# Seven pairs of x sums moved from the windows of a GRU-and-FFN kernel into its setup

## The reference

```python
for t in range(64):                       # B = 64, D = 512
    gi = x[:, t] @ W_ih + b_ih            # 512 x 1536
    gh = h @ W_hh + b_hh
    r = sigmoid(gi_r + gh_r); z = sigmoid(gi_z + gh_z)
    n = tanh(gi_n + r * gh_n)
    h = (1 - z) * n + z * h
    states[:, t] = h
out = x + ffn(states)                     # fp8-rounded operands, gate/up 1408 wide, silu, down
```

## Time and profile before

| | us |
|---|---|
| median of 3 runs | 2847.83 |
| lowest, highest | 2846.3, 2849.53 |
| the profiled execution | 2844.01 |
| its span | 2842.2 |

### The profile page before, as it was taken

One profiled execution on the slowest core, in us unless ns is written; L12 is line 12 of the kernel. 1 busy time (PEld: TensorE's weight loads), 2 busy tenths in 40 slices (PEclk: granted clock), 3 DMA queues, 4 the chain that ended last, 5 costly groups with the idle time before them and its releaser, 6 DMA issues. The chain is left out here.

```text
span 2842.2 us, 154419 instructions
## 1 busy us (share of the span) xinstructions
PE 2554.6 (90%) x67605; PEld 1655.8 (58%) x67605; DVE 1686.3 (59%) x3398; ACT 1139.7 (40%) x2317; POOL 1252.9 (44%) x598
## 2 busy tenths in 40 slices
PE   2088999999989999999999999999896999999996
PEld 1066777777767778777665664755642444444442
DVE  8852222224822222225737879867492888888887
ACT  1312222225722222225602333323233777777774
POOL 0256666663146666665161450713601233333334
PEclk8599999999999999999999999999998999999998
DMA  6833222224622222225664353443432223232322
GB/s 196 241 82 82 71 72 74 71 71 107 146 69 71 72 74 71 71 75 138 191 143 122 109 144 113 125 153 97 146 121 95 71 86 95 79 96 84 95 64 54
DMA packets 234857, 293.97 MB, mean 103 GB/s; under 512 B 69581, under 2 KB 194023, under 8 KB 233895
## 3 DMA queue, kind: packets, MB, share of 16 engines
q1 hardware_dynamic: 212743, 240.84, 31.3%
q10 hardware_dynamic: 18304, 36.19, 3.7%
q0 software_dynamic: 3680, 15.21, 1.9%
HBM read 231.61 MB, written 60.45 MB: 103 GB/s over the span
## 5 line engine op out<-in xcount | busy, mean ns | idle before, releaser
L1161 PE MATMUL psum<-second_shared 64*32 64x384 f16 x32768 | 1029.5, 325 | 48.1 <-issue 28.3
L1169 PE MATMUL psum<-low_w,low_hot 64*32 64x384 f16 x16384 | 819.1, 325 | 5.6 <-issue 5.6
L1407 DVE TENSOR_SCALAR second_shared<-psum 32x384 f16<-32x384 f32 x496 | 272.4, 549 | 754.1 <-PE psum L1161 746.8
L1161 PEld LDWEIGHTS psum<-second_shared 64*32 64x32 f16 x32768 | 594.5, 93 | 209.6 <-issue 78.8
L971 POOL TENSOR_TENSOR low_hot<-first_shared,sum_mask 128x1024 f16<-128x1024 f16 x256 | 504.5, 1971 | 425.0 <-DVE first_shared L1394 165.4
L965 POOL TENSOR_TENSOR second_shared<-first_shared,whole_mask 128x2048 f16<-128x2048 f16 x128 | 462.3, 3612 | 447.3 <-PE psum L1161 352.3
L1061 ACT ACTIVATE second_shared<-psum 32x384 f16<-32x384 f32 x496 | 239.4, 483 | 807.5 <-PE psum L1161 801.5
L1249 PE MATMUL psum<-low_w,low_hot 64*64 64x384 f16 x12288 | 513.9, 325 | 12.6 <-issue 6.5
L1249 PEld LDWEIGHTS psum<-low_w,low_hot 64*64 64x64 f16 x12288 | 373.9, 108 | 146.2 <-issue 10.0
L1169 PEld LDWEIGHTS psum<-low_w,low_hot 64*32 64x32 f16 x16384 | 315.7, 93 | 66.3 <-issue 7.1
L2037 PE MATMUL psum<-first_shared,hT 128*64 128x256 f32 (+1 forms) x1856 | 314.6, 492 | 0.0
(11 more groups left out here) (286 smaller groups left out, 2667.5 us busy)
## 6 DMA issues: line engine op xcount, KB each, us to landing
low_w<-w_rows SPq DMA_DIRECT2D x384, 144.0 KB
low_w<-w_rows SPq DMA_DIRECT2D x256, 120.0 KB
second_shared<-w_rows SPq DMA_DIRECT2D x1024, 24.0 KB, 1.8
x_gates<-x_out ACTq DMA_DIRECT2D x58, 384.0 KB, 2.4
xg<-x_gates SPq DMA_DIRECT2D x58, 384.0 KB, 3.2
low_w<-w_rows SPq DMA_DIRECT2D x256, 72.0 KB
low_w<-w_rows SPq DMA_DIRECT2D x384, 48.0 KB
w_rows<-quantised SPq DMA_DIRECT2D x24, 384.0 KB, 4.9
```

Of the source, the lines that this page charges most:

```text
L1161: last = nc.tensor.matmul(run[m][u][j * Q:(j + 1) * Q, :], whole_hot[rows[u], m, sign, kk, j % 2 * Q:(j % 2 + 1) * Q], whole_w[rows[u], m, ...
L1169: nc.tensor.matmul(run[m][u][j * Q:(j + 1) * Q, :], low_hot[rows[u], m, kk, j % 2 * Q:(j % 2 + 1) * Q], low_w[rows[u], m, at:at + UC], sta ...
L1407: last = nc.vector.tensor_scalar(whole_w[u * B:u * B + Q, m, 0, bq, :], run[m][u][bq * Q:(bq + 1) * Q, :], 1.0 / HIGH_ONE, None, ALU.mult)
```

## The change

Seven of the 29 pairs are made in the setup, with the first four chunks of `raw` as weights and with PSUM banks 1, 3, 4, 5 and 0, after the two plain sums have been taken out of PSUM. The windows keep 5, 6, 5 and 6 pairs. To make room on ScalarE, the 48 loads of operand rows go to SyncE, behind the writes of chunks 2 to 5, and eight activations that fill `whole_a` go from the end of the setup to its start. The first four loads of x rows, which ScalarE issued at the start of the second block, are issued at the start of the kernel. VectorE adds the bias to both plain sums in chunk 0.

```diff
+            X_SETUP = 7
+            SETUP_BANKS = x_banks(1, (3, 4), (5, 0))
# SyncE, setup, in the loop over the chunks n, behind the writes W0, W1, W2
+                            if n == 2:
+                                sp.wait_ge(pieces_out, PIECES_OUT)
+                                load_low(sp, 0, LOW_ROWS, ROWS_X0)
+                            elif n == 3:
+                                load_whole(sp, 0, 0, ROWS_X0)
+                            elif n == 4:
+                                sp.wait_ge(pieces_out, 2 * PIECES_OUT)
+                                load_low(sp, H0, LOW_ROWS, ROWS_H)
+                            elif n == 5:
+                                load_whole(sp, H0, 1, ROWS_H)
# ScalarE, setup
+                        def take_pair(j):
+                            for step in (2 * j, 2 * j + 1):
+                                take_out(a, step, SETUP_BANKS)
+                                if step + 2 < 2 * X_SETUP:
+                                    place_bias(step + 2, SETUP_BANKS)
+                                if step % 2 == 0 and j + 1 < X_SETUP:
+                                    copy_rows(a, j + 1, SETUP_BANKS)
+
+                        for j in range(2):
+                            load_rows(a, j)
+                        a.wait_ge(id_ok, 1)
+                        for m in range(2):
+                            for part in range(2):
+                                own = slice(part * B, part * B + Q)
+                                for bq in range(2):
+                                    nc.scalar.activation(whole_a[own, m, :, bq * Q:(bq + 1) * Q], ident[own, own].unsqueeze(1).to_broadcast([Q, NBK, Q]),
+                                                         ACT.Copy, scale=HIGH_ONE)
...
                             a.wait_ge(w3_ok, n + 1)
                             if n + 2 < CHUNKS:
                                 scale_rows(n + 2)
-                            if n == 2:
-                                a.wait_ge(pieces_out, PIECES_OUT)
-                                load_low(a, 0, LOW_ROWS, ROWS_X0)
-                            elif n == 3:
-                                load_whole(a, 0, 0, ROWS_X0)
...
-                            elif n >= CHUNKS - 2:
...
+                            if n == 0:
+                                copy_rows(a, 0, SETUP_BANKS)
+                                a.wait_ge(x_cleared, 1)
+                                a.wait_ge(bias_ok, 1)
+                                for step in range(2):
+                                    place_bias(step, SETUP_BANKS)
+                            elif n <= X_SETUP:
+                                take_pair(n - 1)
# VectorE, setup, in chunk 0: both plain sums
-                            if c < PLAIN:
-                                v.wait_ge(plain_sum, c + 1)
+                                for n_plain in range(PLAIN):
+                                    v.wait_ge(plain_sum, n_plain + 1)
# TensorE, end of the setup
+                        pe.wait_ge(plain_ok, 2 * PLAIN)
+                        x_pairs(pe, range(X_SETUP), raw[:, 0:KD, :], SETUP_BANKS)
# the windows
-                    return range(X_PAIRS * w // WINDOWS, X_PAIRS * (w + 1) // WINDOWS)
+                    rest = X_PAIRS - X_SETUP
+                    return range(X_SETUP + rest * w // WINDOWS, X_SETUP + rest * (w + 1) // WINDOWS)
# ScalarE, second block
-                        for j in range(2):
-                            load_rows(a, j)
-                            a.wait_ge(x_cleared, t - FINE + 1)
+                            a.wait_ge(x_cleared, t - FINE + 2)
```

More of the change, by code:

```diff
@@ L390, in build @@
                 bias_in = ssem("bias_in")
+                bias_ok = ssem("bias_ok")
                 plain_turned = ssem("plain_turned")
@@ L605, in _ @@
                                 v.wait_ge(bias_in, 64)
-                                nc.vector.tensor_tensor(bias_sum[:], bias[:, 0, 0:2 * HALF], bias[:, 1, 0:2 * HALF], ALU.add)
-                            if c < PLAIN:
-                                v.wait_ge(plain_sum, c + 1)
-                                for at, (tile, part) in enumerate(zip(ps_plain[c % 2], (slice(0, 2 * HALF), slice(2 * HALF, 3 * HALF)))):
-                                    nc.vector.tensor_tensor(gates_plain[:, c, part], tile, bias[:, 0, part], ALU.add).then_inc(plain_ok, 1)
+                                nc.vector.tensor_tensor(bias_sum[:], bias[:, 0, 0:2 * HALF], bias[:, 1, 0:2 * HALF], ALU.add).then_inc(bias_ok, 1)
+                                for n_plain in range(PLAIN):
+                                    v.wait_ge(plain_sum, n_plain + 1)
+                                    for tile, part in zip(ps_plain[n_plain % 2], (slice(0, 2 * HALF), slice(2 * HALF, 3 * HALF))):
+                                        nc.vector.tensor_tensor(gates_plain[:, n_plain, part], tile, bias[:, 0, part], ALU.add).then_inc(plain_ok, 1)
                     @block.tensor
```

## The result

| | before | after |
|---|---|---|
| median of 6 runs, us | 2846.46 | 2861.23 |
| lowest, highest | 2840.84, 2849.53 | 2854.44, 2862.02 |
| the profiled execution | 2844.01 | 2860.68 |
| its span | 2842.2 | 2858.9 |

The changed kernel is 14.8 us slower: the ratio is 1.0054, with an interval of 1.0038 to 1.007. Forecast were 2844.3 and a range up to 2854. It is the second rival's side, and 5 us beyond the rival's own 2856.3.

What follows compares the result with a forecast made beforehand. VectorE's chain was taken to bound the setup and three of four windows, TensorE only the last. +6.0 (setup) - 0.7 (start) + 7.2 (returns) - 16.0 (last window) = -3.5 us, so 2844.3 by median, range 2837 to 2854.

Steps and rivals of the forecast that it cites:

- the second rival: Setup, chunks 4 to 7: full DMA engines make writes land late and VectorE stop; 12 to 20 us, 2856.3; chance 0.18.
- The setup's transfers: Setup: moved x rows and sums add 0.25 to a DMA share of 0.90, so transfers land later; 1.8 us added.
- The whole term of the setup: Setup's end: first x rows, TensorE's new tail and later transfers delay the second block by 6 us, between 4 and 12.
- my three signs of being wrong: Half pair behind the turn at 2.4 GHz, VectorE waiting for writes in the setup, or a pair there over 11.1 us.
- The first x rows: Kernel's start: four loads of 128 KB delay the last weights by up to 1.6 us; 1.3 taken.
- TensorE's tail: Setup: TensorE's seven pairs end at 139.3, so the second block starts at 141.3, 4.2 us later than before.
- The second block's start: TensorE's first product there waits less for its load without the x rows' loads; gain 0 to 2 us, 0.7 taken.
- The three returns of the clock: Steps 2 to 4: after waiting for the state TensorE resumes at 1.2 GHz; 2.4 us each, 7.2 in all.
- The last window: Eight pairs become six, so the block ends with VectorE's state instead of TensorE's sums; gain 15.7 to 16.8 us, 16 taken.
- windows 2 to 4: Windows of steps 2, 3 and 4: VectorE's state ends them, so fewer pairs gain nothing.

Runs made afterwards that it cites:

- small x stores: The changed kernel with the 14 setup stores of x sums cut to 16 of 128 partitions; median 2840.48 us, 0.9982 of the kernel before.
- Full windows: The changed kernel with windows of 7, 7, 7 and 1 pairs instead of 5, 6, 5 and 6; median 2847.7 us, 1.0006 of the kernel before.
- the row loads on SyncE alone: The kernel before with only the 48 row loads moved to SyncE, no x sums in the setup; median 2851.46 us, 1.002 of the kernel before.

## Why the prediction was wrong

**The setup's transfers** are the step that failed: I added 1.8 us for later landings, and took SyncE's late writes "as hidden". The whole term of the setup was +6, and it measured +27.4. The second rival had the mechanism (VectorE stops for `moved`, in chunks 5 to 7, with 20.2 us against its 12 to 20) and its point of decision, a start of 152.3; the start was 164.54. I gave it 0.18. Three readings misled me. I added a share of 0.25 to one of 0.90 and spoke of landings that slip, when the sum says that the bytes don't fit: they take longer, and the writes that VectorE needs stand in the same engines. By my own numbers a share of 1.0 left 8.5 us of the engines' time free in 85, for a need of 20.9: 12.4 us too much, and not the 9 (3 beyond my 6) that I wrote. I gave the landing a spare of 5 to 8 us and took late writes as hidden by it, where chunk 5's writes took 11.6 us from the issue of the last. And I priced SyncE's 16 issues at 0.7 us each, by what they took on ScalarE in a setup without x sums. They took 1.1 us each, so the five spare microseconds were gone before the first write was late. The runs show which is cause and which is effect: the order alone costs nothing (no waits), the order under traffic costs about 6 us, and the stores' traffic taken away leaves 1.4 of 19.7 us. Of my three signs of being wrong, VectorE's waits for writes came, and a pair of more than 11.1 us once (12.1, from 117.01 to 129.13, where TensorE waited for ScalarE); the half pair at 2.4 GHz did not.

The Trainium skill ("DMA: Bandwidth & Descriptors", section "Issuing engines are not separate DMA queues") holds that all issuing engines feed the same 16 DMA engines. The runs agree: moving 48 loads from one queue to another left the start at 137.64. The sentence with it in the prediction put the setup 3 us beyond my 6 if the share could not pass 1.0; from 70 to 130 the largest share of all twelve profiles was 0.94, and a window of 10 us in after reached 0.99.

**The first x rows** were 1.3 us in the sum, by their bytes; they took about 4. Why more than their bytes is not shown.

**TensorE's tail** was right in kind and didn't decide. A pair takes 11.06 us there too (but for the one of 12.1), and the first products are slow (8.35 us for a half pair). The last sums ended at 145.4 instead of 139.3, of which 3.3 are the first x rows' share. The block waited for VectorE. In small x stores, without the waits, the tail does decide, and the setup is then 8.2 us longer than before, against the +6 of the sum.

**The second block's start** was forecast at -0.7. TensorE's wait for the first load went from 8.88 to 7.21 us, 1.7 less. Its first instruction is 27.42 us later than before and the first gates, some 540 us on, are 26.56 us later, so -0.9 is left there.

**The three returns of the clock** were 7.2 us in the sum and took 7.5: the steps from one state to the next grew by 2.1, 3.1 and 2.3. The turns waited 22.36, 11.50 and 22.32, as forecast. Windows of one microsecond behind the turn of step 2 in after (the columns as above):

```profile
1609.00:1610.00 1.00, 0.99 (x4) 0.58 (x6) 0.27 (x1) 0.00 (x0) 0.00 (x0) 0.50 0.03 8
...
1612.00:1613.00 1.00, 1.00 (x6) 0.29 (x4) 0.90 (x4) 0.00 (x0) 0.00 (x0) 0.50 0.00 0
1613.00:1614.00 1.00, 1.00 (x8) 0.51 (x6) 0.93 (x3) 0.00 (x0) 0.00 (x0) 0.83 0.00 0
1614.00:1615.00 1.00, 1.00 (x10) 0.35 (x8) 0.02 (x1) 0.00 (x0) 0.00 (x0) 1.00 0.00 0
```

The clock is 0.50 (1.2 GHz) from the turn at 1609.01 to within the microsecond 1613, 4.3 us, and half of that is lost. Full windows, which take TensorE's idle time away ahead of these turns, give 6.4 us back: the cause is shown. (The other 1.1 is before's own: its step from the state of step 3 to that of step 4 took 180.4 us, where it takes 182.1 in full windows and in the row loads on SyncE alone.) The Trainium skill ("TensorE: Matmul & The Clock Gate", section "HAM oscillation — how this bites in real kernels") has the same mechanism with 1.67 us slow on each return; the trace is 2.6 times that, and taking the trace's figure was right.

**The last window** was forecast at -16 and gave -17.0: 3.6 us from the last state to the third block. That windows 2 to 4 give nothing is shown by the same run of full windows: with seven pairs in each of them the states come no later than with five or six.

**In sum**, by the profiles: +27.4 instead of +6.0, -0.9 instead of -0.7, +7.5 instead of +7.2, -17.0 instead of -16.0. These make +17.0 for the measured +16.7; small differences in untouched stretches (-1.4 and +1.1) make the rest. Had the setup cost its 6, the profile would have been 4.7 us shorter than before, where 3.5 were forecast; the terms outside the setup were right in mechanism and in size.

What stays open: why TensorE stops in step 1 in before and in the row loads on SyncE alone, and why the stretch before step 2 varies by up to 16 us between profiles, a stretch in which 7 to 9 us of the gains of the smaller moves lie by their profiles; how the 20 us of waits split between late issuing and late landing; and why two pairs cost 5 to 7 us in the setup and one pair 1.

## What to carry to other kernels

Before work is moved into a stretch where an engine is idle, work out the bytes that it brings as GB/s and add them to what the DMA engines carry there: no kernel here carried more than 300 GB/s in the setup from 70 to 130, and what was asked beyond it became time on whatever waited for a transfer. Don't judge it afterwards by the mean share, which was 0.87 with 1.4 us of waits and with 25.0. A count of moved work is worth only what ends last in each window: here two pairs out of the last window gave all that seven gave (one pair gave 11.4 of the 17 us), and the other five cost their transfers and three slow returns of TensorE's clock. The three versions that keep TensorE busy up to each turn and move one or two pairs are 0.6 to 0.8% faster than before, where the full move is 0.3 to 0.5% slower; 7 to 9 us of that gain lie, by their profiles, in the stretch that isn't explained.

## What I had not expected of the hardware

Issuing a DMA is not a fixed price: 16 row loads took 9.38 us from SyncE's queue in the setup without the x sums' traffic, 9.90 with an eighth of the stored bytes, and 17.52 with all. In the second block of before, where the share is about 0.5, 16 such loads take 5.66. Four loads of 128 KB at the very start delayed the last of 7.2 MB by about 4 us, where their bytes alone, at the 330 GB/s of the prediction, are 1.6.
